# Issuing the six shifted copies of a row from ScalarE's queue in place of SyncE's

## The chip, the cores and the metric

The kernel runs on one core of a Trainium2 chip. The metric is the device time of one execution in microseconds (us). TensorE is called PE here, VectorE DVE, ScalarE ACT, GpSimd POOL and SyncE SP; a q behind a name means the queue of instructions that this engine issues from, with its DMA issues.

## The reference, cut to what matters

The input is 32 rows (the batch) of 128 x 512 numbers in float32. Each row goes through four residual layers, each with weights or scalars of its own for this row or for all:

```
x = x + einsum(x, W0[subject]) + b0[subject]                      # layer 0
x = x + layernorm(x + relu(x @ W1[lang] + b1) @ W2[lang] + b2)    # layer 1, an adapter
x = x + layernorm((gelu(x @ Wsoma) * sigmoid(temporal @ Wtemp)) @ Wout)   # layer 2, with causal running sums
x = x + L3(x, zX, zY, zR)                                         # layer 3
def L3(y, zX, zY, zR):                                            # dx = dy = 1, edges reflected
    lap_x = left neighbour - 2 y + right neighbour                # along the 512 columns
    lap_y = upper neighbour - 2 y + lower neighbour               # along the 128 rows of time
    return zX * lap_x + zY * lap_y + zR * y * (1 - y)
```

The change touches layer 3 alone. One batch row lies in on-chip memory with its 128 time steps on the 128 partitions, so `lap_y` needs the same data moved by one partition up and by one down.

## The kernel before, in words

The 32 batch rows are worked through as 16 pairs; `p` is a pair, `r` (0 or 1) a row in it, and `b = 2p + r`. The order of each engine's work is written out by hand: each engine runs one loop over `i` from -5 to 16, and in step `i` it does pieces of up to four pairs in different stages, pair `i+3` in layer 0 and the adapter's start, `i+2` in layer 1 and the start of layer 2, `i+1` in the rest of layer 2, and pairs `i` and `i-1` in layer 3 and the store. Engines meet only through semaphores that the program waits on by hand. Every queue is in order: an instruction that waits holds all that stand behind it.

Names in the trace: one large buffer `work` holds most of the tiles, and so nearly everything is `work<-work`; the lines tell the steps apart. The steps that matter, with their lines:

- `x3_row` (DVE L1055) makes `x3`, the input of layer 3 of a row, and signals `x3_ready`.
- `shift_rows` (SP L312) waits for `x3_ready` and for the step `final` of the row before, then issues six DMAs from `x3`: three into `before` (partitions moved by one one way: 112 partitions, 15 partitions and the edge) and three into `after` (the other way). 128 partitions can't be covered by one copy moved by one, and the split in 112 and 15 stands for that.
- `neighbours` (POOL L446, L447) adds the left and right neighbours; `row_neighbours` (POOL L452) waits for all six copies and adds `before` and `after`; `slopes` (ACT L667) follows it, since it writes into `after`; `quadratic` (POOL L457) follows `slopes`; `final_sum` (DVE L1062) follows `quadratic`; `final` (DVE L1068) makes the output tile, and `store` (SP L317) sends it out.
- In layer 2: `soma_gelu` (ACT L635) empties a PSUM bank, and `soma_gelu(p, 3)` that into which PE's second `g_turn` (PE L1351) writes; `state` (PE L1371) stands behind `g_turn`. `gate_tanh` (ACT L653) empties the four gate banks one by one, and PE's `gate_ctx` of the next pair (PE L1241, `wg_r`) waits for the same bank's `gate_tanh`. `relu` (ACT L562) stands before PE's `adapter` (L1283). `w0_hi` (ACT L542) and `w0_lo` (DVE L829) split half a matrix of layer 0 in two parts; both halves land in one buffer, so the load of the next half (SP L247) waits for them. `soma_gate` (DVE L1025) follows `gate_tanh`; `sg_hi` (ACT L661) follows `soma_gate`. `chunk_terms` (DVE L998) makes products, `add_terms` (POOL L416) adds them, and later `chunk_terms` wait for it.

What stands around the step now, on SP: `shift_rows` of a pair's first row (r=0) is issued between a load of half a layer-0 matrix and the loads of b0, x and w2. `shift_rows` of the second row (r=1) stands one step of the loop later, behind loads of x, w1, half of w0, gamma and b1 and ahead of b0, xT and w0. SP reads the subject or language number for each weight load from memory, a few more instructions per load.

Of the kernel before, what the change touches and what calls it, by code (L numbers as in the profile page):

```python
# [5 lines left out]
def cond_resid_kernel(nc, x, xt, subject, language, tau, wn2, bn2, blend, zx, zy, zr, l0_w, l0_b,  # L6
# [11 lines left out]
    P = 128  # L18
# [20 lines left out]
    with ExitStack() as ctx:  # L39
# [165 lines left out]
        def live(p):  # L205
            return 0 <= p < NP
# [20 lines left out]
        def _(sp):  # L227
            with nc.allow_non_contiguous_dma(reason="small constant rows and columns"):
# [72 lines left out]
                        sp.wait_ge(S["x2_ready"], b)  # L301
                    sp.dma_start(xb, l1_beta[language_of(b)].rearrange("l c -> (l c)").partition_broadcast(P)).then_inc(S["beta_loaded"], 16)

                def shift_rows(p, r):
                    b = 2 * p + r
                    sp.wait_ge(S["x3_ready"], b + 1)
                    if b:
                        sp.wait_ge(S["lap_ready"], b)
                        sp.wait_ge(S["fin_ready"], b)
                    for dst, src in ((before[1:EVEN + 1], x3[0:EVEN]), (before[EVEN + 1:P], x3[EVEN:P - 1]), (before[0:1], x3[1:2]),  # L310
                                     (after[0:EVEN], x3[1:EVEN + 1]), (after[EVEN:P - 1], x3[EVEN + 1:P]), (after[P - 1:P], x3[P - 2:P - 1])):
                        sp.dma_start(dst, src).then_inc(S["shifted"], 16)  # L312

                def store(p, r):
                    b = 2 * p + r
                    sp.wait_ge(S["fin_ready"], b + 1)
# [2 lines left out]
                for i in STEPS:  # L319
                    if live(i + 2):  # L320
                        load_x(i + 2, 1)
                        load_w1(i + 2, 1)
                        load_w0(i + 2, 1, 1)
                        load_gamma(i + 2, 0)
                        load_b1(i + 2, 1)
                    if live(i - 1):
                        shift_rows(i - 1, 1)
                    if live(i + 2):
                        load_b0(i + 2, 1)
                    if live(i + 3):  # L330
                        load_xT(i + 3, 0)
                        load_w0(i + 3, 0, 0)
                    if live(i + 2):
                        load_b2(i + 2, 1)
                        load_beta(i + 2, 1)
                        load_w2(i + 2, 1)
                        load_gamma(i + 2, 1)
                    if live(i - 1):
                        store(i - 1, 1)
                    if live(i + 3):  # L340
                        load_w1(i + 3, 0)
                        load_w0(i + 3, 0, 1)
                    if live(i):
                        shift_rows(i, 0)
                    if live(i + 3):
                        load_b0(i + 3, 0)
                        load_x(i + 3, 0)
                        load_w2(i + 3, 0)
                        load_beta(i + 3, 0)
                        load_w0(i + 3, 1, 0)  # L350
                    if live(i):
                        store(i, 0)
                    if live(i + 3):
                        load_xT(i + 3, 1)
                        load_b1(i + 3, 0)
                        load_b2(i + 3, 0)
# [155 lines left out]
        def _(act):  # L512
# [144 lines left out]
            def sg_hi(p, half):  # L657
# [2 lines left out]
                blocks = slice(2 * half, 2 * half + 2)  # L660
                a_.activation(sgh[:, 0, blocks].rearrange("p a r t -> p a (r t)"), gate[:, blocks], ACT.Copy).then_inc(S["sghi_ready"], 1)  # L661

            def slopes(p, r):
                b = 2 * p + r
                act.wait_ge(S["x3_ready"], b + 1)
# [34 lines left out]
            for i in STEPS:  # L700
# [24 lines left out]
                    next_matrix(3)  # L725
                if i == -3:
                    logs()
                if live(i + 1):
                    soma_gelu(i + 1, 3)
                    amat_hi(i + 1, 1)  # L730
                    g_hi(i + 1, 1)
# [24 lines left out]
                    t_hi(i + 1, 1)  # L756
                if live(i + 2):
                    mod_hidden(i + 2)
                if live(i + 1):
                    gate_tanh(i + 1, 0)  # L760
                if live(i + 3):
# [803 lines left out]
```

## Time and profile before

| | before |
|---|---|
| median of 3 runs | 1044.95 us (1042.16 to 1045.16) |
| the profiled execution's own time | 1038.77 us |
| its span, first to last instruction | 1037.0 us |
| busy: PE / DVE / POOL / ACT | 919.3 / 831.4 / 615.0 / 392.7 us |
| granted TensorE clock, mean | 0.970 |
| DMA issues of `shift_rows` | 192 on SP, six for each of 32 rows |
| one pair in the steady part | 58 to 59.5 us |

The busy rows tell which engines are nearly full. The chain of waits tells by which engines the end was set. The timeline of an engine lists what ran and, in brackets, how long the engine stood idle before it and what ended that. In the steady part every pair looks alike, so one pair (500 to 558 us) stands for the others; the second of two variants of it is shown by a few rows from 611 us on.

### The profile page before, as it was taken

The page shows a single profiled execution, that of the slowest core. Times are in us where ns is not written, and L with a number is a line of the kernel's source. Part 1 is how long each engine was busy: PE and PEld are TensorE (multiplying, and loading weights), DVE is VectorE, ACT ScalarE, POOL GpSimd, SP SyncE. Part 2 cuts the span into 40 slices and gives each one's busy share as a digit, 9 for nine tenths or more (in the row PEclk, how much of TensorE's full clock was granted, in tenths as well). Part 3 has the DMA queues.
Part 4 walks back from the last instruction along what each step waited for, and adds up shares of the span by engine and source line. Part 5 has one row for each costly group of instructions (what it writes and reads, how often), then busy time and mean ns, then how long its engine had stood idle before and what let it go on. Part 6 is the DMA issues. An engine that isn't in the chain of part 4 may idle for free.

```text
span 1037.0 us, 18886 instructions
## 1 busy us (share of the span) xinstructions
PE 919.3 (89%) x6088; PEld 776.7 (75%) x6088; DVE 831.4 (80%) x1333; ACT 392.7 (38%) x730; POOL 615.0 (59%) x654
## 2 busy tenths in 40 slices
PE   2678899999899999999999999999999999998961
PEld 1458697878778787878878787887878787887751
DVE  3788779797978979798888979698887969697762
ACT  3463433434243443434343342425343343424220
POOL 1445447484756668484766749475766748474523
PEclk9779999999999999999999999999999999999985
DMA  6664333534343343534454353434344353420011
GB/s 218 214 212 137 108 123 111 165 107 155 115 153 133 116 163 108 158 118 135 129 146 132 122 168 105 155 102 162 124 131 154 104 161 114 141 72 32 31 41 61
DMA packets 92815, 133.28 MB, mean 129 GB/s; under 512 B 15692, under 2 KB 32588, under 8 KB 92716
## 3 DMA queue, kind: packets, MB, share of 16 engines
q1 hardware_dynamic: 88372, 125.93, 38.9%
q10 hardware_dynamic: 4344, 6.14, 1.9%
q8 instruction: 49, 0.80, 0.3%
q14 instruction: 50, 0.41, 0.1%
HBM read 106.86 MB, written 8.39 MB: 111 GB/s over the span
## 4 chain that ended last, share of the span: by engine, by line
DVE 33%; issue 24%; POOL 19%; PE 16%; ACT 3%; DMA 2%; SPq 1%; ACTq 1%; POOLq 0%; DVEq 0%
PE bank L1241 6%; DVE work L998 5%; PE bank L1371 4%; DVE w_r L829 4%; POOL work L416 4%; POOL xh L391 3%; DVE work L1007 3%; POOL b_t L403 2%; PE bank L1233 2%; POOL work L452 2%; DVE work L1014 2%; DMA w_land<-in_L_cond_weight 2%; DVE amath L975 2%; DVE work L1068 2%; POOL work L457 2%
## 5 line engine op out<-in xcount | busy, mean ns | idle before, releaser
L416 POOL TENSOR_TENSOR work<-work 128x448 f32<-128x448 f32 (+3 forms) x224 | 200.3, 894 | 35.4 <-DVE work L998 18.5
L1241 PE MATMUL bank<-x2h,wg_r 128*128 128x256 f32 x1536 | 198.2, 284 | 12.8 <-DVE bank L946 12.8
L1241 PEld LDWEIGHTS bank<-x2h,wg_r 128*128 128x128 f32 x1536 | 185.8, 188 | 27.3 <-DVE bank L946 16.9
L1371 PE MATMUL bank<-gh,amath 128*128 128x512 f32 x384 | 106.1, 412 | 21.7 <-DVE work L998 17.2
L998 DVE TENSOR_TENSOR work<-bank,work 128x512 f32<-128x512 f32 (+7 forms) x256 | 105.1, 446 | 19.5 <-POOL work L416 14.0
L1233 PE MATMUL bank<-w_r,xh 128*128 128x512 f32 x384 | 106.2, 415 | 15.6 <-DVE w_r L829 11.3
L403 POOL TENSOR_TENSOR b_t<-b_t,work 128x512 f32<-128x512 f32 x32 | 51.8, 1618 | 107.9 <-DMA b_t<-in_L_cond_b 66.0
L1241 PE MATMUL bank<-x2h,wsoma_r 128*128 128x256 f32 x768 | 107.5, 289 | 3.7 <-ACT work L615 3.5
L1371 PEld LDWEIGHTS bank<-gh,amath 128*128 128x128 f32 x384 | 68.0, 190 | 55.6 <-DVE amath L975 16.3
L829 DVE TENSOR_TENSOR w_r<-w_land,w_r 128x1024 fp32r<-128x1024 f32 x64 | 85.5, 1337 | 26.6 <-ACT w_r L542 26.6
L1241 PEld LDWEIGHTS bank<-x2h,wsoma_r 128*128 128x128 f32 x768 | 94.4, 188 | 12.7 <-issue 7.2
L1241 PE MATMUL bank<-th,wtemp_r 128*128 128x256 f32 x768 | 100.3, 285 | 2.7 <-DVE th L1021 2.7
L1233 PE MATMUL bank<-wout_r,th 128*128 128x512 f32 x384 | 97.5, 404 | 4.3 <-DVE th L1030 2.4
L1241 PEld LDWEIGHTS bank<-th,wtemp_r 128*128 128x128 f32 x768 | 94.8, 194 | 5.0 <-ACT th L649 2.5
L1233 PEld LDWEIGHTS bank<-w_r,xh 128*128 128x128 f32 x384 | 73.6, 199 | 33.1 <-DVE w_r L829 12.5
L452 POOL TENSOR_TENSOR work<-work 128x512 f32<-128x512 f32 x32 | 49.4, 1544 | 78.3 <-DMA work<-work 78.3
L542 ACT ACTIVATE w_r<-w_land 128x1024 fp32r<-128x1024 f32 x64 | 67.4, 1053 | 51.9 <-DMA w_land<-in_L_cond_weight 51.9
L1233 PEld LDWEIGHTS bank<-wout_r,th 128*128 128x128 f32 x384 | 71.0, 191 | 19.0 <-DVE th L1030 2.6
L1007 DVE TENSOR_TENSOR work<-bank,blend_n 128x512 f32<-128x512 f32 x128 | 82.6, 676 | 2.9 <-PE bank L1371 2.9
L1342 PE MATMUL bank<-ms,vj 128*128 128x192 f32 (+7 forms) x512 | 77.2, 273 | 4.4 <-DVE work L998 4.0
L1342 PEld LDWEIGHTS bank<-ms,vj 128*128 128x128 f32 x512 | 70.4, 193 | 11.0 <-DVE work L998 8.0
L1062 DVE SCALAR_TENSOR_TENSOR work<-work,zt 128x512 f32<-128x512 f32 x32 | 37.1, 1158 | 46.8 <-POOL work L457 46.8
(142 smaller groups left out, 1651.1 us busy)
## 6 DMA issues: line engine op xcount, KB each, us to landing
w_land<-in_L_cond_weight SPq DMA_DIRECT2D x64, 512.0 KB, 3.9
w_t<-in_L_cond_W SPq DMA_DIRECT2D x64, 256.0 KB, 3.2
work<-work SPq DMA_DIRECT2D x64, 224.0 KB, 2.5
work<-in_xT SPq DMA_DIRECT2D x32, 256.0 KB, 3.5
b_t<-in_L_cond_bias SPq DMA_DIRECT2D x32, 256.0 KB, 3.5
work<-in_x SPq DMA_DIRECT2D x32, 256.0 KB, 3.4
work<-in_L_cond_beta SPq DMA_DIRECT2D x32, 256.0 KB, 3.5
b_t<-in_L_cond_b SPq DMA_DIRECT2D x32, 256.0 KB, 3.3
```

The lines of the kernel that those rows point to most:

```text
L403: g_.tensor_tensor(b2_t[:, :], b2_t[:, :], xs[:, r], ALU.add).then_inc(S["xb2_ready"], 1)
L416: g_.tensor_tensor(dst, dst, src, ALU.add).then_inc(S["acc_ready"], 1)
L452: g_.tensor_tensor(before, before, after, ALU.add).then_inc(S["rows_ready"], 1)
L542: a_.activation(w0_r[:, 0, half * CC // 2:(half + 1) * CC // 2], w0_land[:, :, :], ACT.Copy).then_inc(S["w0hi_ready"], 1)
L829: v_.tensor_tensor(w0_r[:, 1, blocks], w0_land[:, :, :], w0_r[:, 0, blocks].bitcast(f32), ALU.subtract).then_inc(S["w0lo_ready"], 1)
L998: ins = v_.tensor_tensor(dst, src, g_q[:, 2 * half:2 * half + 2, :, 0:width], ALU.mult)
L1007: v_.tensor_tensor(u[:, s_], STATES[r][s_][:, :], blend_n[:, :], ALU.mult).then_inc(S["u_ready"], 1)
L1062: v_.scalar_tensor_tensor(nb, nb, zt[:, b, 2:3], after, ALU.mult, ALU.add).then_inc(S["lap_ready"], 1)
L1233: ins = mm(dst, act[:, x_part, a], weight[:, w_part, a], start=(start and a == 0 and x_part + w_part == 0), stop=(stop and a == CC - 1 and ...
L1241: ins = mm(dst, weight[:, w_part, first_block + a, o * P:(o + 1) * P], act[:, x_part, a], start=(not onto and a + w_part + x_part == 0), s ...
L1342: ins = mm(RING[n % 2][:, at_:at_ + 2 * width], vj[:, j, a * P:(a + 1) * P], ms[:, :, 0:width], start=True, stop=True)
L1371: ins = mm(STATES[r][s_][:, :], amath[:, a_part, s_ * P:(s_ + 1) * P], gh[:, g_part], start=(a_part + g_part == 0), stop=(a_part == 1))
```

## The change

`shift_rows` is taken out of SP's loop at both of its places and put into ACT's loop with the same waits and the same six copies. In ACT's step `i`, `shift_rows(i, 0)` stands behind `g_hi(i+1, 0)` and ahead of `soma_gelu(i+1, 3)`; `shift_rows(i, 1)` stands behind `mod_hidden(i+2)` and ahead of `gate_tanh(i+1, 0)`.

```
 SP's loop
-                    if live(i - 1):
-                        shift_rows(i - 1, 1)
-                    if live(i + 2):
                         load_b0(i + 2, 1)
...
-                    if live(i):
-                        shift_rows(i, 0)
-                    if live(i + 3):
                         load_b0(i + 3, 0)
 ACT's loop
+            def shift_rows(p, r):
+                b = 2 * p + r
+                act.wait_ge(S["x3_ready"], b + 1)
+                if b:
+                    act.wait_ge(S["lap_ready"], b)
+                    act.wait_ge(S["fin_ready"], b)
+                for dst, src in ((before[1:EVEN + 1], x3[0:EVEN]), (before[EVEN + 1:P], x3[EVEN:P - 1]), (before[0:1], x3[1:2]),
+                                 (after[0:EVEN], x3[1:EVEN + 1]), (after[EVEN:P - 1], x3[EVEN + 1:P]), (after[P - 1:P], x3[P - 2:P - 1])):
+                    act.dma_start(dst, src).then_inc(S["shifted"], 16)
...
+                if live(i):
+                    shift_rows(i, 0)
                 if live(i + 1):
                     soma_gelu(i + 1, 3)
...
                 if live(i + 2):
                     mod_hidden(i + 2)
+                if live(i):
+                    shift_rows(i, 1)
                 if live(i + 1):
                     gate_tanh(i + 1, 0)
```

The first place, row r=0 in the middle of a step, on ACT after the change. The changed file has other line numbers: L607 is `g_hi`, L655 the six copies, L619 `soma_gelu`, L613 `amat_hi`.

```order
L553 ACTIVATE x2h<-bank 128x4x128
L607 ACTIVATE gh<-bank 128x512
L655 DMA work<-work 112x512
L655 DMA work<-work 15x512
L655 DMA work<-work 1x16x32
L655 DMA work<-work 112x512
L655 DMA work<-work 15x512
L655 DMA work<-work 1x16x32
L619 ACTIVATE work<-bank,cols_t 128x256
L613 ACTIVATE amath<-work 128x512
```

Before, `soma_gelu` came right behind `g_hi` here; now six DMA issues and their wait for `x3` stand between them.

The second place, row r=1 later in the step, on ACT before (L582 `mod_hidden`, L653 `gate_tanh`, L542 `w0_hi`, L562 `relu`, L549 `x_hi`):

```order
L582 ACTIVATE work<-bank,cols_t 128x256
L653 ACTIVATE work<-bank,cols_t 128x256
L542 ACTIVATE w_r<-w_land 128x1024
L562 ACTIVATE work<-bank,b_t 128x128
L549 ACTIVATE xh<-work 128x512
```

and the same place after the change (L566 `mod_hidden`, L637 `gate_tanh`, L526 `w0_hi`):

```order
L566 ACTIVATE work<-bank,cols_t 128x256
L655 DMA work<-work 112x512
L655 DMA work<-work 15x512
L655 DMA work<-work 1x16x32
L655 DMA work<-work 112x512
L655 DMA work<-work 15x512
L655 DMA work<-work 1x16x32
L637 ACTIVATE work<-bank,cols_t 128x256
L526 ACTIVATE w_r<-w_land 128x1024
```

The first `gate_tanh`, and with it all of ACT's work behind it, now waits for the row's `x3` and for six issues.

The same row on SP after the change (L279 the load of b1, L273 of b0, L254 of xT), where the six copies stood between the first two loads:

```order
L279 ISA
L279 DMA b_t<-in_L_cond_b 128x1
L236 TENSOR_LOAD ids_sb
L236 ISA x2
L273 ISA
L273 DMA b_t<-in_L_cond_bias 128x512
L254 DMA work<-in_xT 128x512
```

Nothing else moved on SP; the loads behind the copies simply follow the load of b1.

## Rows read from the trace of the kernel before

**Rows 1.** The page: span, busy time of two engines, the chain by engine.

```profile
span 1037.0 us, 18886 instructions
...
PE 919.3 (89%) x6088; PEld 776.7 (75%) x6088; DVE 831.4 (80%) x1333; ACT 392.7 (38%) x730; POOL 615.0 (59%) x654
...
DVE 33%; issue 24%; POOL 19%; PE 16%; ACT 3%; DMA 2%; SPq 1%; ACTq 1%; POOLq 0%; DVEq 0%
```

**Rows 2.** Waits of the whole run: engine, line, releaser; total us, times, longest.

```profile
ACT work L667 <- POOL work L452: 78.5, 29, 12.5
POOL work L452 <- DMA work<-work: 78.3, 18, 6.2
...
DVE work L1062 <- POOL work L457: 46.8, 16, 8.9
```

**Rows 3.** Timeline of SP's queue, the six copies: start us, length us.

```profile
280.28 5.43 SPq L312 DMA_DIRECT2D work<-work  x6
...
515.69 5.06 SPq L312 DMA_DIRECT2D work<-work  x6
...
543.87 4.21 SPq L312 DMA_DIRECT2D work<-work  x6
```

**Rows 4.** Timeline of DVE: start, length, [idle before, what ended it].

```profile
514.38 1.28 DVE L1055 SCALAR_TENSOR_TENSOR work<-work 128x512 f32<-128x512 f32 x1
...
535.75 0.75 DVE L1055 SCALAR_TENSOR_TENSOR work<-work 128x512 f32<-128x512 f32 x1
...
551.03 0.68 DVE L1030 TENSOR_TENSOR th<-work,th 128x512 fp32r<-128x512 f32 x1
553.42 1.76 DVE L1062 SCALAR_TENSOR_TENSOR work<-work,zt 128x512 f32<-128x512 f32 x1 [1.71 <-POOL work L457]
...
612.88 1.78 DVE L1062 SCALAR_TENSOR_TENSOR work<-work,zt 128x512 f32<-128x512 f32 x1 [3.84 <-POOL work L457]
```

**Rows 5.** Timeline of ACT's queue and ACT early in the run.

```profile
70.48 0.37 ACTq L698 DMA_DIRECT2D work<-in_L_cond_Wout  x1
70.96 0.63 ACT L549 ACTIVATE xh<-work 128x512 fp32r<-128x512 f32 x1
```

**Rows 6.** Timeline of ACT at the first place: the last `soma_gelu`.

```profile
515.49 0.48 ACT L635 ACTIVATE work<-bank,cols_t 128x256 f32<-128x256 f32 x1
```

**Rows 7.** Timeline of PE at the first place.

```profile
518.84 0.60 PE L1351 MATMUL bank<-ident,work 128*128 128x128 f32 x4
520.11 2.34 PE L1371 MATMUL bank<-gh,amath 128*128 128x512 f32 x9 [0.68 <-DVE work L998]
```

**Rows 8.** Timeline of ACT at and behind the second place.

```profile
537.64 0.48 ACT L653 ACTIVATE work<-bank,cols_t 128x256 f32<-128x256 f32 x1 [2.17 <-PE bank L1241]
...
545.11 1.06 ACT L542 ACTIVATE w_r<-w_land 128x1024 fp32r<-128x1024 f32 x1 [2.60 <-DMA w_land<-in_L_cond_weight]
546.07 0.46 ACT L653 ACTIVATE work<-bank,cols_t 128x256 f32<-128x256 f32 x1
...
550.65 0.82 ACT L667 ACTIVATE work<-work,zt 128x512 f32<-128x512 f32 x1 [3.00 <-POOL work L452]
```

**Rows 9.** Timeline of PE behind the second place, in two pairs.

```profile
538.80 1.52 PE L1241 MATMUL bank<-x2h,wg_r 128*128 128x256 f32 x12
...
556.17 3.00 PE L1241 MATMUL bank<-x2h,wg_r 128*128 128x256 f32 x24 [1.04 <-DVE bank L946]
...
611.90 1.64 PE L1241 MATMUL bank<-x2h,wsoma_r 128*128 128x256 f32 x12 [0.90 <-ACT work L615]
...
615.65 3.00 PE L1241 MATMUL bank<-x2h,wg_r 128*128 128x256 f32 x24 [0.74 <-DVE bank L946]
```

**Rows 10.** Timelines of DVE and of POOL: first products of a pair, first additions.

```profile
503.48 1.35 DVE L998 TENSOR_TENSOR work<-bank,work 128x512 f32<-128x512 f32 x3 [0.15 <-PE bank L1342]
...
505.21 8.29 POOL L416 TENSOR_TENSOR work<-work 128x448 f32<-128x448 f32 x8
```

More of the change, by code:

```diff
@@ L302, in load_beta @@
                     sp.dma_start(xb, l1_beta[language_of(b)].rearrange("l c -> (l c)").partition_broadcast(P)).then_inc(S["beta_loaded"], 16)
[L304 to L312, printed above, removed]
                 def store(p, r):
```

## The prediction

> **What bounds the kernel now.** I read the page first, then the whole run's waits, then the timelines of all engines side by side over one pair. PE is busy 89% and DVE 80% of the span, and the chain that ended last is spread over DVE (33%), issue (24%), POOL (19%) and PE (16%) [rows 1]. No engine bounds the kernel alone; PE, DVE and POOL hand work around a ring, with idle pieces under 1 us at most places. ACT and SP hardly stand in the chain, so ACT has idle time, but what it has to do comes due at fixed moments. What the change can save or cost is therefore read at two places per pair, not from the shares.
>
> **What the six copies cost today.** POOL waits 78.3 us in 18 waits for the copies to land, ACT 78.5 us behind it and DVE 46.8 us in 16 waits at final_sum [rows 2]. That is the price of a late start. In the pair from 500 us on, the second row's `x3` is ready at 535.75 + 0.75 = 536.50 [rows 4], but SP starts its six copies at 543.87 [rows 3], 7.4 us later, since loads stand ahead of them. For the first row SP is ready at once: `x3` ends at 514.38 + 1.28 = 515.66 [rows 4] and the issue starts at 515.69 [rows 3]. So only the second row (16 of 32) has something to gain. Of its gain only DVE's wait counts, since ACT and POOL stand idle there anyway: 46.8 / 16 = 2.9 us per pair at the most, 1.71 us in this pair (seven pairs have 1.7 to 2.0 us) and 3.84 us in the pair after it (six have 3.4 to 4.0) [rows 4].
>
> **What the issue costs on ACT.** No row shows an on-chip copy issued from ACT. On SP the six take 4.21 us in most rows, 5.06 and 5.43 in others [rows 3]. On ACT there is a load of 0.37 us that starts at 70.48; the ACTIVATE behind it starts at 70.96, 0.11 us after the issue ends [rows 5]. So an issue does hold the next ACTIVATE where nothing is queued ahead. Six issues at that load's length would be 2.2 us, the low end; 5.4 us is the high end. I take 4.2 us, as these are the same copies and the row of SP is nearest to them. At both places ACT has nothing queued ahead: the wait for `x3` ends later than the work before it.
>
> **First place (r=0).** Now six issues run on ACT from 515.66 to about 519.9. Behind them stands the last soma_gelu, which ran at 515.49 [rows 6] and now runs from 519.95 to 520.4. It empties the bank that PE's second g_turn writes. g_turn started at 518.84 [rows 7]; now it starts at 520.45 and ends 0.60 - 0.1 us later, near 521.0. The nine state matmuls behind it started at 520.11 after an idle wait of 0.68 us for DVE [rows 7]; that wait covers a part, and they now start at 521.0, **0.9 us late**. ACT's amat_hi and DVE's blend_state follow these matmuls, and DVE has no idle time from there to the next `x3`, so nothing wins it back. The place occurs in all pairs but the last: 15 x 0.9 = 13.5 us. At 5.4 us of issue it is 2.1 us (31 us in all), at 2.2 us soma_gelu ends at 518.4 and the cost is nothing.
>
> **Second place (r=1).** Times here are those of the trace, without the 0.9. The issue runs from 536.50 to 540.75. gate_tanh ran at 537.64 [rows 8] and now ends near 541.3. PE's first gate_ctx waits for that bank; it started at 538.80 [rows 9] and now at 541.3, so **PE is 2.5 us late**. Against that stands PE's later idle time: 1.04 us in this pair, 0.90 + 0.74 in the pair after it [rows 9]. PE comes out 1.5 us late in the seven pairs of the first kind and 0.9 us late in the six of the second. The first matmuls of the next chunk, DVE's chunk_terms and POOL's add_terms follow. There DVE's third chunk ends at 503.48 + 1.35 = 504.83 and POOL starts adding at 505.21 [rows 10], so 0.4 us is slack: **1.1 us** remain in the first kind. In the second kind POOL has about 0.7 us of slack, as final_sum's end also comes earlier there, and 0.2 us remain. Two shorter pairs near the end I put at 0.5 each: 7 x 1.1 + 6 x 0.2 + 1 = 10 us.
>
> **Does the early start not win it back?** The copies land about 6 us earlier and row_neighbours no longer waits. But ACT's own work is 3.1 us late: gate_tanh, w0_hi, relu and x_hi all move from 537.64 on by 541.3 - 538.1 = 3.1, and the second w0_hi waits for a load [rows 8] which is released by the first one and DVE behind it, so it moves by as much, from 545.11 to 548.3, and the fourth gate_tanh from 546.07 to 549.2. soma_gate, the DVE step at 551.03 and sg_hi follow; the DVE step now ends near 553.9 (551.03 + 0.68 + 3.1, less some idle time and less the slower steps that POOL's traffic caused) and slopes runs at 550.8 in place of 550.65 [rows 4, 8]. So final_sum ends at 554.7 to 555.2, where it ended at 553.42 + 1.76 = 555.18 [rows 4]. DVE's wait is gone and its work came later by the same amount. In the second kind final_sum ends 1.5 us earlier, which is what its PE and POOL slack above rests on. On SP 4.2 us come free twice a pair; b0 and xT are issued 3 to 4 us earlier, but POOL takes b0 only behind quadratic, and the next w0 load waits for DVE. I cost that at nothing; if POOL's order were not there, nothing would be lost either.
>
> **The sum.** 13.5 + 10 = 23 us over 1038.8 (the profiled execution, span 1037.0) gives 1062; the median of the runs shown is 6 us above that execution, so the number for a median is 1045 + 23 = **1068 us**. A measurement of this kernel can tell about 0.3%, 3 us, from no change.
>
> **A rule against the trace.** The rows have the issue of six small copies at 4.21 us [rows 3], and their start waiting 7.4 us behind other issues in one queue.
> The Trainium skill, DMA: Bandwidth & Descriptors, section "Issuing engines are not separate DMA queues", says that all issuing engines end on the same 16 DMA engines, and that issuing from several "will only save the time on the sequencer it takes to initiate the DMA, which is usually small relative to the DMA itself".
> By that rule the copies get no faster, and with a small issue cost the sum would be the gain of rival A, 10 us faster, in place of 23 us slower; the trace agrees with the first half and not with the "small".
>
> **Rival A: faster, the issue on ACT is short.** At 2.2 to 2.5 us for six, the first place costs nothing. At the second gate_tanh ends near 539.4, PE is 0.6 us late and finds that in its idle time of 1.04 and 1.64 us, while final_sum ends about 2 us earlier. PE then is the bound and is 0.4 us early in one kind and 1.0 in the other: 7 x 0.4 + 6 x 1.0 = 9, some 10 us faster, 1035. For it: the one load on ACT took 0.37. Against it: copies of just this shape take longer on SP. It decides at about 3 us of issue. Chance 0.13.
>
> **Rival B: no change.** Issue near 3.2 us: the first place costs nothing (soma_gelu ends at 519.4, g_turn at 520.0, covered by the 0.68), and the second's 1.5 us on PE is met by its idle time. 1045 +- 3, chance 0.09. It would also come out if ring slack I do not see takes up both delays.
>
> **Rival C: much slower.** The issue on ACT is as slow as SP's slowest rows, 5.4 us, or SP's issues at the same time stretch it. Then the first place costs 2.1 x 15 = 31 us, and the second puts PE 3.7 us late, 2.3 and 1.4 after slack: 7 x 2.3 + 6 x 1.4 + 2 = 26. Sum 57 us, 1102. For it: rows of 5.06 and 5.43. Against: most rows have 4.2. Chance 0.16. That leaves 0.62 for the forecast with issue between 3.7 and 5 us, 1053 to 1086.
>
> **The numbers.** The range reaches from rival B's low side, 1042, to 1093, half way into rival C; it leaves out most of A and about half of C, under 2 in 10. Slower by over 0.3%: 0.62 + 0.16 = 0.78; within: 0.09; faster: 0.13.
>
> **What would show it.** Right: the six issues on ACTq take about 4.2 us at both places, the last soma_gelu runs near 4.4 us after g_hi, g_turn on PE shows a wait for ACT of about 1.5 us before it, and gate_ctx a wait of about 2.5 us for gate_tanh; POOL's 78.3 us wait for copies is nearly gone, DVE's wait at final_sum too, and DVE's wait for gate_tanh has grown by about 3 us a pair. Wrong: issues under 0.5 us apart on ACTq, or PE without new waits at these places while DVE's wait at final_sum is gone (rival A); or PE's waits there while a pair still takes 58 to 59 us, so that slack I have not counted takes them up.

## The result, and the profile after

| | before | changed |
|---|---|---|
| median of four timed runs | 1043.56 us (1039.01 to 1045.16) | 1082.78 us (1077.69 to 1089.54) |
| ratio, 95% interval | | 1.039 (1.032 to 1.045) |
| profiled execution: span | 1037.0 us | 1080.6 us |
| granted TensorE clock, mean | 0.970 | 0.949 |

The changed kernel is 39 us slower, where 23 us were forecast, inside the range of 1042 to 1093. Each ratio here and below is against runs of the kernel before from the same series, whose medians lie between 1040.0 and 1043.6 us. Two executions far above all others of their kernel, one of the kernel before (3100.3 us) and the only one with a trace of the kernel that gets the waits alone (1304.8 us), are used in no ratio and no reading.

In the changed kernel's file the lines are other ones: L655 the copies, L619 `soma_gelu`, L637 `gate_tanh`, L526 `w0_hi`, L1239 PE's `gate_ctx`, L1349 `g_turn`, L1369 `state`, L1053 `x3_row`, L1060 `final_sum`, L436 `row_neighbours`, L1023 `soma_gate`.

The page of the changed kernel: span, busy time, chain by engine and by line.

```profile
span 1080.6 us, 18886 instructions
...
PE 929.9 (86%) x6088; PEld 792.8 (73%) x6088; DVE 832.8 (77%) x1333; ACT 394.9 (37%) x730; POOL 628.1 (58%) x654
...
PE 53%; DVE 17%; ACTq 11%; issue 8%; ACT 4%; POOL 4%; DMA 1%; SPq 0%; POOLq 0%; DVEq 0%
PE bank L1239 30%; ACTq L655 11%; PE bank L1231 9%; PE bank L1340 4%; PE bank L1369 3%; DVE work L1005 2%; PE bank L1281 2%; POOL work L400 2%; DVE work L1012 2%; DVE w_r L827 2%; DVE work L1066 2%; PE bank L1224 2%; PE bank L1274 1%; PE bank L1349 1%; DVE work L1053 1%
```

ACT's queue stood at 1% of the chain before [rows 1]; now the six copies alone are 11% of it. PE's busy time grew by 10.6 us with the same 6088 matmuls, so some of them ran slower.

The whole run's waits of the changed kernel, against [rows 2]:

```profile
DVE work L1023 <- ACT work L637: 90.1, 31, 5.6
...
ACT work L637 <- issue: 76.2, 14, 6.1
...
ACT work L619 <- issue: 61.5, 15, 6.5
...
PE bank L1239 <- ACT work L637: 34.0, 14, 3.1
...
PE bank L1349 <- ACT work L619: 23.8, 15, 2.2
...
POOL work L436 <- DMA work<-work: 15.2, 4, 5.6
...
DVE work L1060 <- POOL work L441: 11.5, 3, 9.0
```

POOL's wait for the copies fell from 78.3 to 15.2 us and DVE's at `final_sum` from 46.8 to 11.5. In their place stand waits for ACT: 14 of PE for `gate_tanh`, 15 of PE for `soma_gelu`, and 90.1 us of DVE for `gate_tanh`. "issue" as the releaser of ACT means that the profile shows nothing that it waited for; here it is its own queue, held by the copies.

ACT at the two places, from its timeline in the changed kernel, against [rows 6] and [rows 8]:

```profile
657.65 0.59 ACT L607 ACTIVATE gh<-bank 128x512 fp32r<-128x512 f32 x1
657.92 4.11 ACTq L655 DMA_DIRECT2D work<-work  x6
662.12 0.47 ACT L619 ACTIVATE work<-bank,cols_t 128x256 f32<-128x256 f32 x1 [3.88 <-issue]
...
679.57 4.10 ACTq L655 DMA_DIRECT2D work<-work  x6
683.72 0.47 ACT L637 ACTIVATE work<-bank,cols_t 128x256 f32<-128x256 f32 x1 [5.20 <-issue]
```

Six issues take 4.1 us on ACT, as long as on SP [rows 3], and the next ACTIVATE starts 0.05 to 0.1 us after the last.

PE at the two places of the same pair, from its timeline, against [rows 7] and [rows 9]:

```profile
662.74 0.63 PE L1349 MATMUL bank<-ident,work 128*128 128x128 f32 x4 [1.52 <-ACT work L619]
663.13 2.33 PE L1369 MATMUL bank<-gh,amath 128*128 128x512 f32 x9
...
684.25 2.93 PE L1239 MATMUL bank<-x2h,wg_r 128*128 128x256 f32 x12 [2.24 <-ACT work L637]
686.97 1.81 PE L1239 MATMUL bank<-th,wtemp_r 128*128 128x256 f32 x12
```

Both waits are those of the prediction. The last two rows hold what it had not: the 12 matmuls of `gate_ctx` took 2.93 us, where [rows 9] have 1.52, and the 12 behind them 1.81.

The same stretches of the changed kernel by windows (us of the window, its length, busy time by engine, granted clock, DMA share, GB/s):

```profile
681.90:684.20 2.30, 0.10 (x1) 0.00 (x0) 0.00 (x0) 0.48 (x2) 0.00 (x0) 0.97 0.69 215
684.20:687.00 2.80, 2.75 (x13) 2.76 (x14) 1.65 (x2) 2.44 (x5) 1.67 (x1) 0.50 0.75 201
687.00:692.20 5.20, 5.20 (x39) 4.72 (x39) 2.52 (x4) 1.84 (x3) 4.16 (x5) 0.96 0.47 157
```

PE did next to nothing for 2.3 us and then worked 2.8 us at a granted clock of 0.50, which is 1.2 of 2.4 GHz. Before, PE had no such wait here. Such a slow stretch followed 12 of the 14 waits: in ten of these pairs the `gate_ctx` right behind the wait took 2.3 to 2.93 us, and in two (1.79 and 1.95 us) the slow matmuls were the 12 behind it, at 2.76. At the first place it came in two of 15 pairs, in the nine `state` matmuls behind `g_turn`:

```profile
352.24 0.63 PE L1349 MATMUL bank<-ident,work 128*128 128x128 f32 x4 [1.70 <-ACT work L619]
352.62 3.89 PE L1369 MATMUL bank<-gh,amath 128*128 128x512 f32 x9
```

**Where the 43.6 us of span came from.** I took the times between one `x3_row` and the next in both traces. From the first row's to the second row's (which holds the first place) the 16 pairs sum to 13.7 us more; from there to the next pair's (which holds the second place) to 30.1 us more. Together 43.8 us, the whole growth of the span. The first sum is 0.8 us in each of ten pairs, about 2 us in each of the two with the slow stretch, 2.6 us in the last three together, and 1.1 us less in one pair, in which the kernel before had itself taken 2 us longer than elsewhere.

### The profile page after: what moved, and what is told of

The parts are those of the page before. It is cut to its first block, busy times and chain, and to the rows that moved or that the text cites. A ratio compares the mean times of both kernels' runs of the same rounds, so it can differ in the third digit from the quotient of the medians.

```text
span 1080.6 us, 18886 instructions
## 1 busy us (share of the span) xinstructions
PE 929.9 (86%) x6088; PEld 792.8 (73%) x6088; DVE 832.8 (77%) x1333; ACT 394.9 (37%) x730; POOL 628.1 (58%) x654
## 4 chain that ended last, share of the span: by engine, by line
PE 53%; DVE 17%; ACTq 11%; issue 8%; ACT 4%; POOL 4%; DMA 1%; SPq 0%; POOLq 0%; DVEq 0%
PE bank L1239 30%; ACTq L655 11%; PE bank L1231 9%; PE bank L1340 4%; PE bank L1369 3%; DVE work L1005 2%; PE bank L1281 2%; POOL work L400 2%; DVE work L1012 2%; DVE w_r L827 2%; DVE work L1066 2%; PE bank L1224 2%; PE bank L1274 1%; PE bank L1349 1%; DVE work L1053 1%
## 5 line engine op out<-in xcount | busy, mean ns | idle before, releaser
L1239 PE MATMUL bank<-x2h,wg_r 128*128 128x256 f32 x1536 | 213.1, 297 | 37.3 <-ACT work L637 34.0
L1239 PEld LDWEIGHTS bank<-x2h,wg_r 128*128 128x128 f32 x1536 | 200.4, 200 | 50.2 <-ACT work L637 37.3
L1231 PE MATMUL bank<-w_r,xh 128*128 128x512 f32 x384 | 105.8, 414 | 17.4 <-DVE w_r L827 11.5
L1369 PE MATMUL bank<-gh,amath 128*128 128x512 f32 x384 | 108.1, 419 | 8.0 <-issue 4.1
L1239 PE MATMUL bank<-th,wtemp_r 128*128 128x256 f32 x768 | 105.5, 294 | 2.7 <-DVE th L1019 2.7
L1239 PE MATMUL bank<-x2h,wsoma_r 128*128 128x256 f32 x768 | 106.1, 288 | 0.0
L1023 DVE SCALAR_TENSOR_TENSOR work<-work 128x256 f32<-128x256 f32 x64 | 35.9, 562 | 90.1 <-ACT work L637 90.1
L1239 PEld LDWEIGHTS bank<-th,wtemp_r 128*128 128x128 f32 x768 | 101.0, 204 | 5.0 <-ACT th L633 2.5
L1239 PEld LDWEIGHTS bank<-x2h,wsoma_r 128*128 128x128 f32 x768 | 94.1, 188 | 7.2 <-issue 7.2
L1369 PEld LDWEIGHTS bank<-gh,amath 128*128 128x128 f32 x384 | 70.1, 196 | 36.0 <-DVE amath L973 18.9
L619 ACT ACTIVATE work<-bank,cols_t 128x256 f32<-128x256 f32 x64 | 30.3, 474 | 168.6 <-PE bank L1239 107.1
L526 ACT ACTIVATE w_r<-w_land 128x1024 fp32r<-128x1024 f32 x64 | 67.3, 1052 | 41.3 <-DMA w_land<-in_L_cond_weight 41.3
L441 POOL TENSOR_TENSOR work<-work 128x512 f32<-128x512 f32 x32 | 53.0, 1657 | 43.3 <-ACT work L661 43.3
```

Of the source, the lines that this page charges most:

```text
L441: g_.tensor_tensor(after, slope, x3, ALU.mult).then_inc(S["quad_ready"], 1)
L526: a_.activation(w0_r[:, 0, half * CC // 2:(half + 1) * CC // 2], w0_land[:, :, :], ACT.Copy).then_inc(S["w0hi_ready"], 1)
L1231: ins = mm(dst, act[:, x_part, a], weight[:, w_part, a], start=(start and a == 0 and x_part + w_part == 0), stop=(stop and a == CC - 1 and ...
L1239: ins = mm(dst, weight[:, w_part, first_block + a, o * P:(o + 1) * P], act[:, x_part, a], start=(not onto and a + w_part + x_part == 0), s ...
L1369: ins = mm(STATES[r][s_][:, :], amath[:, a_part, s_ * P:(s_ + 1) * P], gh[:, g_part], start=(a_part + g_part == 0), stop=(a_part == 1))
```

## The experiments

The edits are shortened: lines with `if live(...)` and unchanged lines are left out where they tell nothing.

### One place at a time

The first row's copies on ACT and the second row's on SP; and the other way round.

```
 first only: ACT, step i                 second only: ACT, step i
+                if live(i):            +                if live(i):
+                    shift_rows(i, 0)   +                    shift_rows(i, 1)
                     soma_gelu(i+1, 3)                       gate_tanh(i+1, 0)
```

> Only the first row's (r=0) six copies go to ACT's queue; the second row's stay on SP at their old place. Theory (ACT's queue is held 4.1 us and the work behind it comes late): the two x3 of a pair stand 22.17 us apart in place of 21.36, so 0.8 us a pair plus a slow-clock stretch in two of 15 pairs, some 14 us in all, ratio to the kernel before 1.013; g_turn waits 1.5 us for the last soma_gelu. Rival 1 (the loss comes from the copies running in a second DMA queue beside SP's loads): the loss is shared by copies, half of 39 us = 20 us, ratio 1.019, without a wait of PE for soma_gelu. Rival 2 (the first place is free): ratio 1.00.

> Only the second row's (r=1) six copies go to ACT's queue. Theory: PE waits 2.2 to 3 us for gate_tanh in 14 pairs and then runs the matmuls behind the wait at half clock; what is left of the 39 us after the first place's 14 is 25 us, ratio 1.024, mean granted clock near 0.955. Rival 1 (second DMA queue): 20 us, 1.019. My prediction's own term without the clock: 10 us, 1.010.

Measured: 1.016 (1.009 to 1.022) for the first place alone, 1.025 (1.019 to 1.030) for the second alone. They add up to 1.041, within the interval of the changed kernel's 1.039. The second DMA queue as the cause would have made them equal; the intervals overlap at 1.019 to 1.022, so the ratios alone don't exclude it, but the waits do: each kernel has PE's wait for ACT at its own place and none at the other. Two rows from the PE timelines, the first of the first-only kernel and the second of the second-only one:

```profile
533.51 0.63 PE L1360 MATMUL bank<-ident,work 128*128 128x128 f32 x4 [1.72 <-ACT work L632]
```

```profile
370.64 2.93 PE L1250 MATMUL bank<-x2h,wg_r 128*128 128x256 f32 x12 [2.67 <-ACT work L650]
```

In the second-only kernel five of the 14 `gate_ctx` behind that wait took 2.6 to 2.93 us and two more 2.3, and in another two the slow stretch came just behind; its mean clock was 0.956, the first-only kernel's 0.961. The expected two slow stretches of the first place were six of 15 in the first-only kernel, one of them in this pair:

```profile
350.71 1.09 PE L1360 MATMUL bank<-ident,work 128*128 128x128 f32 x4 [1.88 <-ACT work L632]
```

There the stretch with the first place grew by 20.9 us in the profiled execution, against 13.7 in the changed kernel.

### The waits without the issues

The six copies stay on SP; ACT gets only the semaphore waits of `shift_rows` at the two places.

```
+            def shift_rows(p, r):
+                b = 2 * p + r
+                act.wait_ge(S["x3_ready"], b + 1)
+                if b:
+                    act.wait_ge(S["lap_ready"], b)
+                    act.wait_ge(S["fin_ready"], b)
```

> All six copies stay on SP as before; ACT gets the waits of shift_rows at the changed kernel's two places and issues nothing. It separates the wait for x3 on ACT from the time its queue is held by the issues. Theory: x3 is ready 0.1 us after g_hi at the first place and 1.1 us before gate_tanh runs at the second, so the wait costs nothing: ratio 0.998 to 1.002, no wait of PE for soma_gelu or gate_tanh. Rival (the order alone costs, since ACT can't run ahead of x3): 1.005 to 1.02.

Measured: 1.000 (0.998 to 1.003). The wait for `x3` on ACT costs nothing. What costs is the queue's time for the issues. That PE has no new waits here follows from the total alone; no trace of this kernel is read.

### PE kept busy while it would wait

The changed kernel, and PE runs the 12 matmuls of the second `gate_part` twice.

```
 def gate_part(p, a):
+                if a == 1:
+                    cols_times(GATES[a][:, 0:W2], wtemp_r, th_cols, 0, a)
                 cols_times(GATES[a][:, 0:W2], wtemp_r, th_cols, 0, a).then_inc(S["gate_done"], 1)
```

> The changed kernel, and PE does the 12 matmuls of gate_part for the second bank twice (the first time over, same result): 1.4 us of extra PE work per pair, inside the 2.2 us in which PE waits for gate_tanh. Theory that the clock falls because PE stands idle there: the wait shrinks to 0.9 us, the 12 gate_ctx matmuls behind it take 1.5 us in place of 2.9, and the kernel is faster than the changed one although it does more: 14 pairs x 1.2 to 1.7 us = 17 to 24 us less, near 1062, ratio to the kernel before 1.018. Rival (the slow stretch comes from what runs beside it, or the wait alone costs the time): no faster than the changed kernel, 1083 or, where the extra work reaches past the wait, above; ratio 1.038 or more.

Measured: 1.033 (1.028 to 1.039), 1076.0 us, against 1082.8: with 192 matmuls more it is no slower and in the medians 7 us faster, though the two intervals overlap, so the total alone doesn't settle it. The PE timeline of this kernel does:

```profile
683.20 1.65 PE L1239 MATMUL bank<-x2h,wg_r 128*128 128x256 f32 x12 [1.12 <-ACT work L637]
684.69 1.52 PE L1239 MATMUL bank<-th,wtemp_r 128*128 128x256 f32 x12
```

and by windows (columns as above):

```profile
682.10:683.20 1.10, 0.00 (x0) 0.00 (x0) 0.02 (x1) 0.52 (x2) 0.38 (x1) 1.00 0.85 286
683.20:684.70 1.50, 1.50 (x13) 1.50 (x14) 1.50 (x2) 1.50 (x3) 0.90 (x1) 1.00 0.71 211
```

With the wait down to 1.1 us the matmuls behind it ran at a clock of 1.00, in 13 of 14 pairs in 1.63 to 1.68 us. The DMA engines were about as busy beside these matmuls (0.71, against 0.75 in the slow stretch of the changed kernel), which speaks against the traffic as the cause. The stretch with the second place grew by 15.2 us over before in place of 30.1: half of the second place's cost was the slow clock. Why the total gained only 7: the slow stretches came up at the first place instead, where PE waits 1.5 us as before. In five pairs the four `g_turn` matmuls took over 1 us there in place of 0.63, in two more the nine `state` matmuls behind them took 3.89 in place of 2.3, and that stretch grew by 20.1 us in place of 13.7.

```profile
660.20 1.09 PE L1351 MATMUL bank<-ident,work 128*128 128x128 f32 x4 [1.52 <-ACT work L619]
```

So the theory of the clock holds for its place, and the expected 17 to 24 us were not got.

### Three copies on each queue, at the old places of SP and the new ones of ACT

```
 ACT: shift_rows at the changed kernel's places, with
+                for dst, src in ((before[1:EVEN + 1], x3[0:EVEN]), (before[EVEN + 1:P], x3[EVEN:P - 1]), (before[0:1], x3[1:2])):
 SP: shift_rows where it stood, with
+                for dst, src in ((after[0:EVEN], x3[1:EVEN + 1]), (after[EVEN:P - 1], x3[EVEN + 1:P]), (after[P - 1:P], x3[P - 2:P - 1])):
```

> Both rows: the three copies into `before` from ACT at the changed kernel's places, the three into `after` from SP at the old places. Theory: ACT is held 2.1 us. At the first place soma_gelu ends near 518.3 on the old time scale, ahead of g_turn, and costs nothing; at the second gate_tanh is 1 us late, PE waits 0.5 us and keeps its clock, and the six have landed 2 us earlier than before, so DVE's wait at final_sum (1.7 or 3.8 us) shrinks by up to 2: between 5 us slower and 10 us faster than the kernel before, ratio 0.990 to 1.005. Rival 1 (second DMA queue): half the copies on it, 20 us slower, 1.019. Rival 2 (the loss goes with the held time in proportion): 1.019 too, with a wait of PE for gate_tanh of 1 us or more.

The copies into `before` are issued by ACT at the changed kernel's places, those into `after` by SP where all six stood.

Measured: 0.998 (0.995 to 1.001). ACT held for 2.1 us twice a pair costs nothing net that can be told, although 96 copies go through the second queue. The second queue as the cause should have cost 1.9% here. The copies also land a little earlier (DVE's wait at `final_sum` is 28.8 us in place of 46.8), which may hide a small cost; the kernels below, faster than the kernel before the change with 48 or 96 copies in ACT's queue, leave little of that rival.

### The short issue of rival A

```
-EVEN, N_SHIFT = P - 16, 6
+EVEN, N_SHIFT = P - 16, 3
 ACT's shift_rows: the three copies into before only
-g_.tensor_tensor(before, before, after, ALU.add)
+g_.tensor_tensor(before, before, x3, ALU.add)
```

> Leaves out the three copies into `after` (row_neighbours adds x3 in their place); the three into `before` are issued from ACT at the changed kernel's two places. So ACT is held 2.1 us and all copies land early: this is the short issue of the prediction's rival A. Theory: first place free, second place 1 us late on gate_tanh and 0.5 us on PE, DVE's wait at final_sum gone: 5 to 10 us faster than the kernel before, ratio 0.990 to 0.996. If the early landing is worth nothing (PE bounds there): ratio 0.998 to 1.003 as with three copies on each queue. If any issue on ACT in a starved place costs its length: 1.01 or more.

This kernel leaves out the three copies into `after`, so it does not compute `lap_y` as the reference does, and only its time is of use. Measured: 0.974 (0.969 to 0.979), 27 us faster, much more than the 5 to 10 expected. DVE's waits in this kernel (first three rows, and `final_sum` is L1059):

```profile
DVE work L1022 <- ACT work L637: 60.1, 28, 3.8
DVE w_r L826 <- ACT w_r L526: 26.2, 18, 12.3
DVE work L910 <- PE bank L1280: 22.3, 13, 2.3
...
DVE work L1059 <- POOL work L441: 9.4, 3, 6.8
```

An early landing is worth more than I had allowed it: I had taken PE's idle time as its ceiling. This kernel and the one before it hold ACT for the same 2.1 us and differ by 24 us; here every copy lands early, and there are fewer of them. The kernels below tell that the early landing, and not the missing copies, is most of it.

### The second row's copies later on ACT

First row on SP. Second row's six on ACT, behind `mod_scaled`, where ACT was idle.

```
                     mod_scaled(i + 2)
+                if live(i):
+                    shift_rows(i, 1)
```

> First row's copies on SP as before; second row's six on ACT, but behind mod_scaled, that is behind three of the four gate_tanh, where ACT stood idle 2.6 us for a load. Theory: gate_ctx on PE no longer waits and the clock stays (0.97); the second w0_hi and the fourth gate_tanh come 1.7 us late, the copies land when they did before: within 8 us of the kernel before, ratio 0.998 to 1.008. Rival (second DMA queue, or SP's order): as slow as the second place alone was, 1.024.

Measured: 1.015 (1.008 to 1.021). That is above the expected 1.008, and below the 1.025 of the same copies ahead of `gate_tanh`. No `gate_ctx` waits now. But the copies are issued at the end of ACT's idle time and the second `w0_hi` and the fourth `gate_tanh` come late; DVE waits for that one, and still waits at `final_sum`:

```profile
489.30 3.56 ACTq L668 DMA_DIRECT2D work<-work  x5
492.97 1.06 ACT L539 ACTIVATE w_r<-w_land 128x1024 fp32r<-128x1024 f32 x1 [3.56 <-DMA w_land<-in_L_cond_weight]
```

```profile
494.42 0.43 DVE L1034 SCALAR_TENSOR_TENSOR work<-work 128x256 f32<-128x256 f32 x1 [1.80 <-ACT work L650]
...
501.24 1.77 DVE L1071 SCALAR_TENSOR_TENSOR work<-work,zt 128x512 f32<-128x512 f32 x1 [1.71 <-POOL work L454]
```

The row names the w0 load as what released `w0_hi`. But that load was issued at 487.89 and, by the median of 3.7 us from issue to landing, was there near 491.6 (an estimate), while the last issue ended at 489.30 + 3.56 = 492.86, 0.1 us before `w0_hi` ran: it was the queue. ACT's idle time of 2.6 us is shorter than the 4.1 us of six issues, and I had costed the rest too low.

### The same copies early, on SP

SP's order for the second row was x, w1, the half w0, gamma, b1, the six copies. It is now x, three copies, the half w0, three copies, then gamma, w1 and b1.

```
                         load_x(i + 2, 1)
+                        shift_rows(i - 1, 1, slice(0, 3))
+                        load_w0(i + 2, 1, 1)
+                        shift_rows(i - 1, 1, slice(3, 6))
+                        load_gamma(i + 2, 0)
                         load_w1(i + 2, 1)
-                        load_w0(i + 2, 1, 1)
-                        load_gamma(i + 2, 0)
                         load_b1(i + 2, 1)
-                        shift_rows(i - 1, 1)
```

> Nothing on ACT. On SP the second row's copies are moved forward: three behind the load of x, then the load of half a w0, then the other three, then gamma, w1 and b1. Copies land at about 546.5 on the scale of the trace before in place of 549.2, no load that is waited for comes more than 0.5 us late. Theory that DVE's wait at final_sum is worth what PE leaves (1.0 and 1.6 us of idle per pair): 5 to 15 us faster, ratio 0.986 to 0.995. Rival (the ring has other bounds): 0.998 to 1.003.

Measured: 0.990 (0.987 to 0.993), 1030.7 us. With nothing on ACT the earlier copies give 1%. The loads moved with them do not explain it, since the w0 load comes later after `x3` (5.3 us, before 4.6) and so do gamma, w1 and b1. From its DVE timeline: `final_sum` (L1065) no longer waits, and the fourth `soma_gate` does.

```profile
543.22 1.28 DVE L1028 SCALAR_TENSOR_TENSOR work<-work 128x256 f32<-128x256 f32 x1 [1.84 <-ACT work L656]
...
549.17 1.79 DVE L1065 SCALAR_TENSOR_TENSOR work<-work,zt 128x512 f32<-128x512 f32 x1
```

### Both queues, three each, ACT's behind mod_scaled

```
 SP                                             ACT
                         load_x(i + 2, 1)                     mod_scaled(i + 2)
+                        shift_rows(i - 1, 1, slice(0, 3))  +     shift_rows(i, 1), the copies into after
+                        load_w0(i + 2, 1, 1)
                         load_w1(i + 2, 1)
-                        load_w0(i + 2, 1, 1)
...
-                        shift_rows(i - 1, 1)
```

> First row as before. Second row: three copies from SP behind the load of x, as in the kernel with the early copies on SP, the other three from ACT behind mod_scaled, where ACT has 2.6 us idle and is held 2.1. Theory: both queues issue in time they had idle; same as or 2 us better than the early copies on SP alone, ratio 0.984 to 0.995. Rival: any issue on ACT costs, 1.005 or more.

Measured: 0.992 (0.989 to 0.996), the same as the copies early on SP within the intervals. Neither better nor worse: three issues fit into ACT's idle time.

### The number read ahead of the copies

As early on SP, and the subject number for the w0 load is read before the copies.

```
+                        subject_b = subject_of(2 * (i + 2) + 1)
                         shift_rows(i - 1, 1, slice(0, 3))
-                        load_w0(i + 2, 1, 1)
+                        load_w0(i + 2, 1, 1, subject_b)
```

> The kernel with the early copies on SP, and the subject number for the half w0 load is read before the first three copies, so the load follows them without the 0.8 us that the read takes. In the kernel without it that load came 0.7 us later after x3 than in the kernel before and DVE waited 1.8 us for the fourth gate_tanh behind it. Theory: 0.5 us or more per pair: 6 to 10 us faster than with the early copies alone, 1022 to 1026, ratio 0.980 to 0.985. Rival (PE bounds the ring there, so the load's lateness was covered): same as the early copies alone, 0.990.

Measured: 0.985 (0.983 to 0.988), 1025.3 us. The w0 load is issued 4.9 us after `x3` in place of 5.3. Half a percent better than without, at the edge of what was expected; the two intervals just meet (0.987).

### Three on each queue, both early

First row as before. Second row: three copies on ACT ahead of `gate_tanh`, three on SP behind the load of x.

```
 SP, against the kernel of the section above    ACT
-    shift_rows(i - 1, 1, slice(0, 3))          +    shift_rows(i, 1), the copies into before
+    shift_rows(i - 1, 1, slice(3, 6))               gate_tanh(i + 1, 0)
     load_w0(i + 2, 1, 1, subject_b)
-    shift_rows(i - 1, 1, slice(3, 6))
```

> First row as before. Second row: three copies from ACT at the changed kernel's second place (held 2.1 us) and at the same time the other three from SP behind the load of x, with the subject number read ahead. All land about 3 us earlier than with SP alone, at the cost of gate_tanh 1 us late. Theory: DVE's wait at final_sum was gone already, so the earlier landing brings nothing more and the held ACT costs 0.5 us of PE: 0 to 8 us slower than the kernel with the read ahead, ratio 0.982 to 0.992. Rival (what the short issue on ACT won, 27 us, was won by the early landing): 0.973 to 0.980.

Measured: 0.978 (0.975 to 0.980), 1018.5 us, 23 us faster than the kernel before the change, 7 us faster than the kernel of the section above, and the fastest that computes everything. The rival's number, not mine. It holds ACT as long at the second place as three copies on each queue at the old places did, has all six copies in time, and is 2% faster. SP's order and the first row's queue differ too, but the difference lies in the stretch with the second place: against before it took 14.4 us less in the profiled execution, where three on each queue at the old places took 2.5 more. Of these 17 us the read ahead has a part (about 5 us by the two kernels on SP); the rest I take to be the landing, since the held time is the same. PE now waits 6.1 us in all for `gate_tanh` in ten waits, and its clock stays:

```profile
472.81 1.65 PE L1254 MATMUL bank<-x2h,wg_r 128*128 128x256 f32 x12 [0.93 <-ACT work L655]
```

### Five on ACT and one on SP

```
 SP:   shift_rows(i - 1, 1, slice(5, 6)) in place of slice(3, 6)
 ACT:  the first five of the six copies in place of the first three
```

> As the kernel with three copies early on each queue, but five of the second row's copies on ACT (held 3.4 us) and one on SP. The landing is early in both, so what differs is the held time. Theory: PE waits 1.5 to 1.8 us for gate_tanh in place of 0.6; where that wait leaves the clock at 1.00 the kernel loses 1.3 us a pair less what idle time PE still has, 8 to 18 us against the kernel with three: 1027 to 1037, ratio 0.985 to 0.996. If a wait of this length already halves the clock behind it, 1.4 us a pair more: 1045 to 1055, ratio 1.003 to 1.013. Rival (the held time is free until it meets some other bound): no more than 3 us above the kernel with three.

Measured: 1.006 (1.004 to 1.008), 1045.8 us, 27 us above the kernel with three on ACT (29 by the ratios) for 1.5 us more of held time (3.5 in place of 2.0) in each of 14 pairs, 21 us. From its PE timeline:

```profile
368.89 2.93 PE L1255 MATMUL bank<-x2h,wg_r 128*128 128x256 f32 x12 [2.22 <-ACT work L655]
...
607.38 1.65 PE L1255 MATMUL bank<-x2h,wg_r 128*128 128x256 f32 x12 [1.65 <-ACT work L655]
...
725.59 1.70 PE L1255 MATMUL bank<-x2h,wg_r 128*128 128x256 f32 x12 [1.86 <-ACT work L655]
727.11 2.75 PE L1255 MATMUL bank<-th,wtemp_r 128*128 128x256 f32 x12
```

The waits are 1.6 to 2.9 us. The `gate_ctx` behind them took 1.64 to 1.88 us in 12 pairs and 2.46 and 2.93 in the two others; in three of the 12 the slow stretch came in the 12 matmuls behind `gate_ctx`, as in the last row (2.75 in place of 1.52). So it followed five of 14 waits. The time lies at the low end of the expectation's second case, but not for that case's reason, a slow clock in every pair: 21 us are the held time and some 7 us the clock (an estimate: in the rows 1.70 + 2.75 against 1.65 + 1.52 is 1.3 us, for each of five stretches). I had PE's idle time take up some of the held time, and by this sum it took up nothing, as far as is shown because the earlier `final_sum` had used it already.

## Why the prediction was right, and where it was off

- **The issue on ACT takes 4.2 us: right.** 4.10 to 4.99 us, in most rows 4.1. Rival A (short issue) and rival C (5.4 us) fall with it. That an issue holds the next ACTIVATE is shown by the changed kernel's rows and not by [rows 5]: beside that load an ACTIVATE (`relu`) ran over the same 0.37 us.
- **First place, 0.9 us a pair, 13.5 us: right in the mechanism, the sum in part by luck.** 0.8 us in ten pairs, 13.7 us over the profile. `g_turn` waits 1.52 us, as foreseen. Two pairs cost 2 us, from slow matmuls behind that wait, and one pair less because the kernel before had been slow in it. With more slow stretches the same place cost 20 us (the kernel with the extra matmuls) and 21 (the first place alone, where the ratio says 1.6%, 0.9 to 2.2).
- **Second place, the wait of PE: right.** 2.0 to 3.1 us for `gate_tanh` in 14 pairs, forecast 2.5.
- **Second place, the sum: the failing step.** "PE is 2.5 us late" was taken as all there was, and 10 us came out of it; the profile has 30. The term left out, put at nothing without a reason, is the granted clock: behind 12 of the 14 waits a slow stretch came, in ten of them with `gate_ctx` at 2.3 to 2.93 us, where 1.65 is a run behind a short wait. The pairs of the first kind cost 2.5 us on average (forecast 1.1), those of the second 1.5 (forecast 0.2), and the last two together 4.0 (forecast 1). Keeping PE busy took 15 of the 30 away: the first kind then cost 1.3, the second 0.8 and the last two 1.4. So the sum was near right for the first kind once the clock is taken out; for the second the 0.7 us of slack on POOL was too much. The new wait should have been followed by the question what the clock does behind it; the kernel before has no wait of PE for `gate_tanh` at all, so the rows of its steady part show no price for it.
- **The range.** 1082.8 lies in it, and in the forecast's own 1053 to 1086, but that width was meant for issues of 3.7 to 5 us and, above it, for rival C's 5.4. The issues took 4.1 and the missing 16 us came mostly from the clock, so that the range held is partly luck.
- **"The early start wins nothing back": right in the sum, wrong as a ceiling.** In the changed kernel ACT's lateness did take its place: POOL's and DVE's waits for copies went, and DVE's wait for `gate_tanh` grew from 42.1 to 90.1 us. But the early landing is worth 15 to 20 us when ACT is held for 2.1 us only (0.978 against 0.998, of which the read ahead may have 5), not the 10 of rival A. I had read PE's 1.0 and 1.6 us of idle time as its limit. Those idle pieces are waits for DVE, and they move when DVE comes earlier.
- **Slack.** Subtracting it from a delay of PE and adding the early landing's gain to it used the same idle time twice; the kernel with five copies on ACT shows a delay there passed on in full, as far as its sum can tell.
- **The decision point.** The text put it near 3 us of held time. With early landing, and at the second place alone, it lies between 2.0 (0.978) and 3.5 us (1.006), by a straight line near 3.2 (an estimate).
- **The rule.** Six issues of small copies took 4.1 us on ACT as on SP, held the ACTIVATEs behind them as long, and the copies landed no faster (median of the largest 2.6 us after the issue, on SP 2.5). The Trainium skill, DMA: Bandwidth & Descriptors, section "Issuing engines are not separate DMA queues", says that issuing from several engines only saves the sequencer's time to initiate the DMA, "which is usually small relative to the DMA itself". The first half agrees with the runs; "small" does not, with 4.1 us of issue for six copies against 2.6 to landing.

## What to carry to other kernels

Moving DMA issues to an engine that looks idle costs the issue time at the moment they are due, not on average: read what stands behind them in that queue, and how soon its consumer wants it. Here ACT could give 2 us and not 4, so the way to start the copies earlier was to split them over two queues and to move them ahead of loads that nobody waits for yet. Where a delay makes TensorE wait for about 2 us, look at the duration of the matmuls behind the wait as well as at the wait.

## What the runs showed that I had not expected

- Behind waits of 2.2 us in the changed kernel `gate_ctx` mostly took 2.93 us (granted clock 0.50), but in the last pairs 1.65 and 1.69 us behind waits of 2.16 and 2.01. In the first-only kernel waits of 1.86, 1.88 and 2.90 us were followed by `g_turn` at 1.09 us in place of 0.63, and three waits of 1.51 to 1.58 us, as long as others that nothing followed, by a slow stretch just behind (nine `state` matmuls at 3.8 to 3.9 us in place of 2.3). Which waits are followed by the lower clock stays open; the runs do not give a length that decides it.
- 12 more matmuls per pair made the stretch with the second place 15 us cheaper over the run, and the stretch with the first place 6 us dearer.
- Six small copies take 4.1 us to issue on either queue, 0.68 each. Size makes little difference: five of them take 3.5, so the sixth, of 2 KB, takes 0.6. Their data landed some 2.5 us after the issue (median).
- Not tried: fewer copies that still move everything (the split in 112 and 15 partitions is not forced by the shift, which only needs the edge apart; four copies might do), and the first row's copies split over the two queues along with the second row's.
